# First pass of a two-pass attention block: layer norm of the input by centred weights, a raw copy on ScalarE and a product on GpSimd

## The reference, cut to what matters

```
def _ln_c(v, eps=1e-6):
    m = jnp.mean(v, axis=1, keepdims=True)
    s = jnp.var(v, axis=1, keepdims=True)
    return (v - m) / jnp.sqrt(s + eps)
...
qkv = jnp.einsum('bcxy,oc->boxy', x, w_qkv)      # x is _ln_c(x)
q, k, v = jnp.split(qkv, 3, axis=1)
...
q = jax.nn.softmax(q, axis=-2) * scale           # over the 32 channels of a head
k = jax.nn.softmax(k, axis=-1)                   # over the 16384 tokens
v = v / n
context = jnp.einsum('bhdn,bhen->bhde', k, v)
out = jnp.einsum('bhde,bhdn->bhen', context, q)
...
x = x + _L0_conv_ref(_ln_c(x), L0_conv_w_qkv, L0_conv_w_out, L0_conv_b_out, L0_conv_g)
```

## Time and profile before

| | |
|---|---|
| median of 3 runs | 5960.17 us (5957.18 to 5989.16) |
| the profiled execution's own time | 5967.46 us |
| its span | 5965.6 us |
| mean granted clock of TensorE | 0.961 of full speed |
| PE busy, PEld busy | 91%, 77% of the span |
| DVE, ACT, POOL busy | 69%, 74%, 57% of the span |

### The profile page before, as it was taken

The page is one execution under the profiler, slowest core; times in us unless marked ns, Lnnn a source line. Parts: engine busy times, 40 slices in busy tenths (PEclk is TensorE's granted clock), DMA queues, the critical chain, the costliest instruction groups (busy, mean ns, idle before and its releaser), DMA issues. The chain is left out here.

```text
span 5965.6 us, 151143 instructions
## 1 busy us (share of the span) xinstructions
PE 5439.1 (91%) x39038; PEld 4617.2 (77%) x39038; DVE 4101.7 (69%) x14529; ACT 4443.4 (74%) x12440; POOL 3416.7 (57%) x5129
## 2 busy tenths in 40 slices
PE   8898989899999999998989898999997999999996
PEld 7777777777777777777777777777776888888885
DVE  7786877777787878787878787777874334434332
ACT  7787878888888888787878788888884555556554
POOL 4655565656565565656565656565652555566554
PEclk9999999999999999999999999999998999999998
DMA  2616162625344352626161626353445477778876
GB/s 67 173 53 176 50 182 62 169 86 146 108 125 129 102 155 78 173 61 177 53 176 50 182 66 167 89 142 112 122 133 177 136 204 207 213 212 223 227 193 148
DMA packets 1690867, 820.74 MB, mean 138 GB/s; under 512 B 1094563, under 2 KB 1622819, under 8 KB 1688355
## 3 DMA queue, kind: packets, MB, share of 16 engines
q1 hardware_dynamic: 1688998, 816.80, 48.9%
q10 hardware_dynamic: 1584, 0.79, 0.0%
HBM read 413.17 MB, written 270.01 MB: 115 GB/s over the span
## 5 line engine op out<-in xcount | busy, mean ns | idle before, releaser
L423 ACT ACTIVATE y<-bank,zbias 128x128 f32<-128x128 f32 x2176 | 798.4, 367 | 564.6 <-PE bank L389 471.0
L489 POOL TENSOR_TENSOR x_t<-x_t,y 128x512 f32<-128x512 f32 x512 | 766.2, 1520 | 630.5 <-ACT y L423 630.5
L445 DVE TENSOR_TENSOR th_t<-x_t,bank 128x512 f32<-128x512 f32 x544 | 544.1, 1040 | 830.5 <-PE bank L360 830.5
L739 ACT ACTIVATE xhT<-bank,nmr,rstd 128x128 f32<-128x128 f32 x2048 | 770.7, 459 | 311.0 <-POOL nmr L826 306.8
L389 PE MATMUL bank<-y,VT 128*128 128x128 f32 x4344 | 957.9, 303 | 10.2 <-issue 9.7
L367 PE MATMUL bank<-th_t,WzT 128*128 128x128 f32 x4352 | 832.8, 278 | 10.1 <-DVE th_t L445 10.0
L389 PEld LDWEIGHTS bank<-y,VT 128*128 128x128 f32 x4344 | 652.1, 190 | 165.6 <-issue 132.0
L689 PE MATMUL bank<-MT,qin 128*128 128x128 f32 x4096 | 636.6, 304 | 139.8 <-ACT onT L795 129.6
L689 PEld LDWEIGHTS bank<-MT,qin 128*128 128x128 f32 x4096 | 541.0, 207 | 228.1 <-issue 107.7
L781 ACT ACTIVATE thT<-bank,srstd 128x128 f32<-128x128 f32 x2048 | 584.4, 369 | 128.1 <-POOL srstd L851 105.1
L367 PEld LDWEIGHTS bank<-th_t,WzT 128*128 128x128 f32 x4352 | 657.6, 194 | 16.3 <-DVE th_t L445 16.3
(11 more groups left out here) (129 smaller groups left out, 11661.3 us busy)
## 6 DMA issues: line engine op xcount, KB each, us to landing
xin<-in_x SPq DMA_DIRECT2D x512, 256.0 KB, 2.8
x2in<-in_x SPq DMA_DIRECT2D x512, 256.0 KB, 3.1
qin<-q_image SPq DMA_DIRECT2D x512, 256.0 KB, 3.0
x_scratch<-x1o SPq DMA_DIRECT2D x1024, 128.0 KB, 2.2
out<-x_t SPq DMA_DIRECT2D x256, 512.0 KB, 6.5
r_t<-r_scratch SPq DMA_DIRECT2D x17, 96.0 KB
r_scratch<-rS ACTq DMA_DIRECT2D x3, 256.0 KB, 22.5
r_scratch<-rS SPq DMA_DIRECT2D x3, 256.0 KB, 21.9
```

Of the source, the lines that this page charges most:

```text
L423: act.activation(y[c][:, g % RING, u, :], z_b[c][g % 2][:, u * CC:(u + 1) * CC], ACT.Sigmoid, bias=zbias[:]).then_inc(y_sb[c], 1)
L445: dve.tensor_tensor(th_t[c][:, g % 2].rearrange("p u (x q) -> p u x q", x=XP), x1_t[q][:, c * CC:(c + 1) * CC, h * GS:(h + 1) * GS].rearra ...
L489: pool.tensor_tensor(dst, dst, y[c][:, g % RING, :, :].rearrange("p u (x q) -> p q x u", x=XP), ALU.add).then_inc(slot_free[c], 1)
L739: i = act.activation(xhT[:, S.slot(1, 4), t, :], xT_b[p][:, t * C:(t + 1) * C], ACT.Identity, bias=nmr[:, p, t:t + 1], scale=rstd[:, p, t: ...
```

## The change

The rows of the q, k and v weights are centred once in the setup (DVE, three instructions), so the mean of a token need no longer be subtracted. POOL no longer makes `mr` and `nmr`. ACT copies the raw transposed chunk s from its bank to a new tile `xTs` in one instruction, in step s itself, when the `bn_stats` of chunk s are done (`x_bn`), and POOL multiplies it with `rstd` in one product of 128 x 512, in step s too, ahead of `qhT`. PE may overwrite the bank once the copy is made (`xT_sb`).

```diff
@@ PE setup
+            pe.wait_ge(qkv_mid, 1)
...
@@ PE step
                     if S.has(2):
-                        pe.wait_ge(ln, S.upto(2))
+                        pe.wait_ge(xT_sb, S.upto(2))
...
@@ ACT step
-                if S.has(1):
-                    act.wait_ge(stat, S.upto(1))
-                    if S.has(5):
-                        act.wait_ge(g_ps, S.upto(5))
-                    p = S.slot(1, 2)
-                    for t in range(TL):
-                        i = act.activation(xhT[:, S.slot(1, 4), t, :], xT_b[p][:, t * C:(t + 1) * C], ACT.Identity,
-                                           bias=nmr[:, p, t:t + 1], scale=rstd[:, p, t:t + 1])
-                    i.then_inc(ln, 1)
+                if S.has(0):
+                    act.wait_ge(x_bn, S.upto(0))
+                    if S.has(2):
+                        act.wait_ge(ln, S.upto(2))
+                    act.copy(xTs[:, S.slot(0, 2), :], xT_b[S.slot(0, 2)][:]).then_inc(xT_sb, 1)
...
@@ POOL step
-                    if S.has(2):
-                        pool.wait_ge(ln, S.upto(2))
+                    if S.has(1):
+                        pool.wait_ge(ln, S.upto(1))
                     pool.wait_ge(x_var, S.upto(0))
                     pool.tensor_tensor(rstd[:, p, :], veps[:, 0, :], minus_half[:], ALU.pow).then_inc(x_rstd, 1)
                     pool.wait_ge(x_rstd, S.upto(0))
-                    pool.tensor_tensor(mr[:], mv[:, p, :, 0], rstd[:, p, :], ALU.mult).then_inc(x_mr, 1)
-                    pool.wait_ge(x_mr, S.upto(0))
-                    settle(pool)
-                    pool.tensor_scalar(nmr[:, p, :], mr[:], -1.0, None, ALU.mult).then_inc(stat, 1)
+                    pool.wait_ge(xT_sb, S.upto(0))
+                    if S.has(4):
+                        pool.wait_ge(g_ps, S.upto(4))
+                    pool.tensor_tensor(xhT[:, S.slot(0, 4), :, :], xTs[:, p, :].rearrange("n (t c) -> n t c", c=C),
+                                       rstd[:, p, :].unsqueeze(2).to_broadcast([C, TL, C]), ALU.mult).then_inc(ln, 1)
...
@@ DVE setup
+            chain(dve.tensor_reduce(w_mean[:], wqkv_in[:], AX, ALU.add))
+            chain(dve.tensor_scalar(w_mean[:], w_mean[:], 1.0 / C, None, ALU.mult))
+            dve.tensor_tensor(wqkv_in[:], wqkv_in[:], w_mean[:].unsqueeze(2).to_broadcast([C, 3, C]), ALU.subtract).then_inc(qkv_mid, 1)
...
@@ DVE step
                     if S.has(2):
-                        dve.wait_ge(stat, S.upto(2))
+                        dve.wait_ge(x_rstd, S.upto(2))
```

More of the change, by code:

```diff
@@ L98, in build @@
         x_in = [sem(f"x_in{i}") for i in range(4)]
-        xT_ps, x_bn, x_mv, x_var, x_rstd, x_mr, stat, ln = (
-            sem(s) for s in ("xT_ps", "x_bn", "x_mv", "x_var", "x_rstd", "x_mr", "stat", "ln"))
+        xT_ps, xT_sb, x_bn, x_mv, x_var, x_rstd, ln = (
+            sem(s) for s in ("xT_ps", "xT_sb", "x_bn", "x_mv", "x_var", "x_rstd", "ln"))
         xh_ps, xh_sb, k_ps, kc_max, k_max, ek_sb, ekT_ps, ekT_sb, g_ps, z_upd, g_upd = (
@@ L113, in build @@
                              "s_rstd", "gram_ps", "s_kept", "thT_sb"))
-        W_mid = sem("W_mid")
+        W_mid, qkv_mid = sem("W_mid"), sem("qkv_mid")
         x1_st = [sem(f"x1_st{i}") for i in range(4)]
@@ L166, in build @@
         rstd = sa("rstd", [C, 2, TL])
-        nmr = sa("nmr", [C, 2, TL])
-        mr = sa("mr", [C, TL])
+        w_mean = sa("w_mean", [C, 3])
+        xTs = sa("xTs", [C, 2, CH])
         xhT = sa("xhT", [C, 4, TL, C])
```

## The result

The changed kernel takes 6224.05 us (median of 4 runs, 6219.68 to 6239.95) against 5973.39 us before (5957.18 to 5989.16): a ratio of 1.0425, 95% interval 1.0384 to 1.0466. It is **251 us slower**. The forecast was 6190 us, range 6115 to 6265, slower with 0.93. It was built on a median before of 5960 us, from three runs; so 13 of the 34 us between 6190 and 6224 are a higher value before, and 21 are the change (251 against 230).

A forecast was written before the change was run, and what follows sets the result against it. The prediction took a wait loop through ACT's exp and PE's L657 as the bound. Steady steps 202, mixed steps 36, drain -8 and setup 1 gave 231 us: 6198 on the profiled execution, 6190 as median, range 6115 to 6265.

The forecast's parts named there:

- start of ACT's exp after X, plus 1.71, plus 1.46: First-pass step length: wait until exp, 1.71 us from exp to PE's L657, 1.46 from there to the next X.
- X: The start of a step's x transposes on PE, from which times within the step are counted.
- PE's own: The 4.40 us of the short first-pass step, in which PE is never held up; the least a step takes.
- The change on ACT: First pass: the copy waits for its own step's bn_stats, exp at X + 2.06, step 5.25 us, 202 us slower.
- jitter of two equal loops: First pass: routes from L657 to bn_stats through DVE (2.08) and PE (2.10) are equal; lateness adds 0.02 us a step.
- The change on POOL: First pass: the 1.05 us product makes qhT end 0.43 later, 0.99 into the next step, but this hides.
- cover: Slack up to PE's L657: qhT may come 0.7 us later than forecast before the delay costs.
- The mixed steps and the drain: Steps 1 to 4, the first three mixed with the second pass: +36 us; step 32, without a copy: -8 us.
- B: Rival: POOL's delay of qhT counts, up to 0.22 us a step, 91 us, time 5960 to 6050; chance 0.04.
- C: Rival: relief of ACT wins, the step falls to PE's 4.40 us, 152 us faster, time 5810; chance 0.04.
- E: Rival: PE's granted clock falls to its lower level in a tenth of steps, 87 us more, time 6280; chance 0.04.
- A: The forecast itself: ACT's loop through bn_stats sets the step, 6190 us, own range 6138 to 6260; chance 0.87.

The follow-up runs named there:

- e5: The changed kernel with ACT's raw copy at the head of its step made twice, the first into an unread tile: 6478 us.
- e4: The kernel before with the centred weights alone: no mr and nmr, ACT keeps its four activations but only scales: 5778 us.
- e7: The changed kernel with ACT's raw copy and POOL's product one step later, on chunk s-1: 5817 us.
- e2: The changed kernel with only POOL's order changed, qhT made before the product: 6234 us.
- e8: The changed kernel with POOL's product made twice, the first into an unread tile: 6271 us.
- e1: The changed kernel with ACT's raw copy moved from the head of its step to behind the ekT copy: 5993 us.
- e3: The changed kernel with both moves, ACT's copy behind the ekT copy and POOL's qhT before the product: 5838 us.

## Why the prediction was right, point by point

**What bounded the kernel before.** The sum "start of ACT's exp after X, plus 1.71, plus 1.46" was read from two steps of one trace. The after trace gives 2.05 + 1.71 + 1.43 = 5.19, and e5 adds the dose to the first term alone: for the changed kernel the sum is shown. For the kernel before it is read from the trace. e4 brings the step to 4.39, the 4.40 that the prediction called PE's own, but it shortens two routes at once: what stands before the exp on ACT, and with `mr` and `nmr` also the way to `qhT`. It does not tell which of the two held the long steps; no run did. What the change cost does not hang on that.

**The change on ACT.** Right by mechanism, and every time within 0.04 us in a plain step. The hand-over that the prediction put at 0.05 "at the least" was 0.03 here (`bn_stats` end at 402.74, the copy starts at 402.77). What was mis-sized is the mean: 5.28 and not 5.25. It was not the jitter of two equal loops. Three steps in four take 5.18 to 5.24, the fourth 5.52; in the fourth `bn_stats` start 0.85 after X and not 0.64, and the copy 0.16 after their end and not 0.03:

```profile
459.10 0.65 PE L623 MATMUL bank<-ident,xin 128*128 128x128 f32 x4
...
459.95 0.89 DVE L925 BATCH_NORM_STATS2 bn<-bank 128x6 f32<-128x128 f32 x4 [0.19 <-PE bank L623]
...
461.00 0.58 ACT L738 COPY xTs<-bank 128x512 f32<-128x512 f32 x1 [2.16 <-DVE bn L925]
```

So "all alike" was not borne out, and that the mean came so near the forecast is in part luck: the plain steps were shorter than 5.23 and the fourth longer. The loop's body holds four steps, so the fourth is the one that comes with the jump back. With it the term was +217.5 and not +202. That the jump is the cause is argued from the period alone; no run took it away. In e4 and e7, where PE is the limit, the steps are all 4.39 and it does not show.

**The change on POOL.** Right: `qhT` was forecast to end 0.99 into the next step and ends at 1.04, the product takes 1.04 (forecast 1.05), and it hides. e2 takes 1.05 us away and gains nothing; e8 adds 1.05 and the steady step does not notice. The cover was larger than the 0.7 us I gave it. The Trainium skill, GPSIMD Engine Reference, section "Elementwise", has some 2.6 cycles an element at 1.2 GHz for such a product, from which 1.11 us is an estimate; the trace has 1.04. In the changed kernel the product hides in the steady steps; in e1, where ACT's wait is gone, `qhT` is the limit at 4.78 us and e3 wins 0.34 a step by putting it ahead of the product.

**The mixed steps and the drain.** +43.4 against +36, -4.4 against -8: the right signs, both sizes estimates between wide bounds. Steps 0 to 3 took 1.18 us an image more (forecast 1.2), step 4 took 1.71 more (forecast 1.24). In the two of images 2 to 15 in which the clock stayed at 1.00 in step 4, that step took 7.64 and 7.66 us, in all fourteen 8.15 on the mean: by this estimate 0.5 us an image, 7 us in all, go with the clock. That ACT's other work stands behind a `bn_stats` there too is borne out by e5, whose extra 0.48 us costs 2.2 us an image in steps 0 to 5.

**The rivals.** B was refuted by e2 and e8 as the cause of the loss, and is true as the limit behind it (e1 against e3). C, that the relief of ACT wins, failed at the point that was named for it: the exp would have to start at X + 1.25, and it starts at X + 2.05. The Trainium skill, Perfetto Trace Analysis, section "Identifying the Most-Contended Engine", has one optimise the engine of the highest occupancy first. Taken by itself that misleads here: ACT's share fell by 26 points and the kernel became slower, and e5 shows that ACT's idle time is not to be had. It is not refuted either, since e4 relieves ACT too (83.03 us of work for some 20.5 steps, 4.05 a step, against 4.34) and is faster. The clean case is e7: with the instructions of the changed kernel (ACT 3.56 us a step, 3.42 there) it takes 4.39 us a step and not 5.28, so what decides is what stands in front of the work and not its amount. E, the clock, came true in a small part, though only A was needed for the number. The clock stayed at 1.00 in the steady stretch with PE 88% busy, against E; but around steps 4 to 7 of most images it fell below full, which the prediction had named as a sign of being wrong. The price is small: some 7 us in step 4 and, from the lengths of steps 5 to 8 against the later ones, some 5 us behind it, 12 of 260 by estimate. No run held the clock fixed.

## What to carry to other kernels

In this pipeline the head of ACT's step was the dearest place in it: a wait put there was a wait for everything behind it, and the same copy two places further down cost 231 us less (e1). Before an instruction is moved to a new place, ask which step's data it will wait for, and add up from there to the next engine; if the sum closes on itself within one step, it is the step. Here the instruction that read what another engine had just worked on did better a lag later (e7), or behind the work that was ready (e1).

An idea and its placement are two changes: the centred weights alone were worth 3.3%, and the kernel that carried them was 4.2% slower.

## What the runs showed that was not expected

The steady first pass can run at PE's own 4.39 us, with PE busy through the whole of a 90 us stretch (e4, 340 to 430) while ACT is busy 83.03 us and DVE 85.74 us of it:

```profile
340.00:430.00 90.00, 90.00 (x696) 78.84 (x695) 85.74 (x319) 83.03 (x225) 46.69 (x61) 1.00 0.19 56
```

Three engines were busy for 92% and more of it side by side, while the changed kernel, with ACT at 65%, was 0.9 us a step slower.

Four scalings without a bias (e4, `ACT.Copy` with `scale`) take 368 ns each, where the kernel before had 458 ns for `ACT.Identity` with scale and bias of each token, on the same tiles. Function and bias were changed together, so the runs alone leave open which of them makes the 90 ns. The Trainium skill, ScalarE: Activation LUTs, section "What ACT_TABLE_LOAD costs", gives about 93 ns for each per-partition operand of an ACTIVATE and about 93 ns by which two in a row overlap. The first agrees with the 90 ns, the second roughly with the copies of e5, which last 0.59 us and start 0.48 apart, an overlap of 0.11.
